# Silu of the deferred experts from Tanh on ScalarE and two products on VectorE, their banks in VectorE's ring

## The chip, the core and the metric

The kernel runs on one core of a Trainium2 chip. The metric is the device time of one execution in microseconds (us), less is better. The core's engines are TensorE (PE in the profile; its weight loads are PEld), VectorE (DVE), ScalarE (ACT) and GpSimd (POOL); SyncE (SP) issues all DMAs here. Each engine works through its own list of instructions in order and waits on semaphores.

## The reference

Four samples of 512 rows by 128 pass through four gated residual blocks. Only the last one is touched by the change: a mixture of 64 experts, the best 8 of them per row, plus two shared ones.

```
def body(acc, p):                                   # for each of 64 routed experts, w1: 128 x 32, w2: 32 x 128
    h = jax.nn.silu(xf @ W1 + B1) @ W2 + B2
    cw = jnp.sum(jnp.where(ti == e, tw, 0.0), axis=-1)    # the row's weight for expert e, 0 if not among its 8
    return (acc + cw[:, None] * h, None)
def shared_mlp(W1, B1, W2, B2):                     # two of them, hidden width 256
    return jax.nn.silu(xf @ W1 + B1) @ W2 + B2
x = x + jnp.tanh(g_ffn[1]) * (routed + shared)
```

Before that block come cross attention to 154 context rows, two layers of local attention with a gelu feed-forward, and a self and cross attention layer with a relu feed-forward. All values are float32.

## The kernel before, in words

Two slots hold two samples at a time: samples 0 and 1 first, then 2 and 3. The experts of samples 0 and 1 are **deferred**: they are computed while samples 2 and 3 go through their attention layers. Samples 2 and 3 compute theirs at once, at the end of the kernel, with another code path that the change leaves alone (L934, `weigh` at L1291).

The hidden units of all experts, turned so that units lie on partitions and the 512 rows along the free dimension, make 20 chunks of 128: chunks 0 to 3 are the shared experts, chunks 4 to 19 the routed ones, four experts of 32 units each. For a deferred sample u and a chunk c:

- PE multiplies the chunk's first weights with the sample's input (`expert_hidden`, L595) into a bank of PSUM.
- ACT applies Silu with the bias (L959) and writes `units[c % 3]` in SBUF.
- For a routed chunk DVE multiplies that by the rows' weights (L1284), which SP has broadcast from DRAM into `ahead[k % 2]`, one DMA for each of four experts (`fill_ahead`, L1628).
- PE multiplies by the second weights and adds up in `moe_psum` (`expert_out`, L605), two steps after the hidden chunk. In the last step the bias of the routed experts is added by one more matmul, ACT scales the sum with the gate (`expert_sum`, L950), PE turns it back (L623), DVE adds x (L1288) and SP stores it.

**The order** is written out once and is the same on all engines. Each stream (slot 0, slot 1, the deferred experts) is a generator of steps, and `turns` (L78) lays down whose step comes next: while samples 2 and 3 are under way, a step of the deferred stream follows about every three steps of the slots. Each engine runs the same sequence of steps, so its place in its own list is fixed; nothing is decided at run time. In step c of the deferred stream PE fills chunk c and takes chunk c-2, ACT does chunk c, DVE multiplies chunk c-1, and SP waits for that product and refills its buffer.

**Banks.** PSUM has eight banks: three in ACT's ring (`act_bank`, L397), four in DVE's (`dve_bank`, L405), one for `moe_psum`. PE takes the banks of a ring in turn. Before it writes a bank it waits until the engine of the ring has emptied the bank's last item, counted by one semaphore per ring, so items of a ring are emptied in order. Hidden chunks are items of ACT's ring. Local attention takes two DVE banks for the scores of a tile, cross attention four.

What else runs in those steps: local attention's scores are masked and their peaks found on DVE (L1111), the negative peaks (L1171, L1224) release eight exponentials on ACT (L847), DVE inverts the sums (L1098), and POOL divides (L1489); PE turns the weights into one bank of each ring, copied by DVE (L1177 or L1230) and ACT (L830). The rotation of queries and keys is L1130 and L1134 on DVE, behind squares on ACT (L858). A feed-forward uses Gelu on ACT (L1001) and a product on DVE (L1358). ACT's table of functions has to hold the function that it applies; the compiler puts ACT_TABLE_LOAD instructions in its list where it has to change.

## Time and profile before

| | |
|---|---|
| three runs | 979.61, 972.08, 977.14 us; median 977.14 |
| profiled execution | 978.57 us, of which the span of instructions is 976.8 us |
| busy, share of the span | PE 75%, DVE 57%, ACT 55%, PEld 49%, POOL 31% |
| mean granted clock of TensorE | 0.868 of full speed |
| ACT_TABLE_LOAD by line | L847 x21, L959 x21, L1001 x8, L838 x2, L1040 x2, L943 x2, L970 x1, L1015 x1; each 1283 ns |
| chain that ended last, share by engine | PE 40%, DVE 26%, ACT 22%, POOL 4%, issue 4% |

A load of the table stands under the line of the instruction that follows it. Busy time says how much an engine did, not that it held up the end; for that the chain of waits is read. It is followed back from the last instruction, at each step to what released it or to the instruction before it on its engine. "issue" is time in which an engine waited for nothing that the profile shows. The profiler doesn't count semaphore and DMA-issuing instructions as busy.

### The profile page before, as it was taken

The numbers are of one execution on the slowest core, as the hardware profiler recorded it, in microseconds if no ns is written. First come the engines' busy times: TensorE is split into PE (matmuls) and PEld (weight loads), VectorE is DVE, ScalarE is ACT, GpSimd is POOL, SyncE is SP. The second block draws the span as 40 slices with busy tenths as digits, with TensorE's granted clock in tenths as the row PEclk, the third lists the DMA queues.
The fourth block names the chain that finished last, engine by engine and source line by source line (L and its number), as shares of the span: only waits on it lengthen the run. The fifth ranks groups of instructions, "written<-read, shape, count | busy, mean of one in ns | idle before, by whom it ended". The sixth has DMA issues, their size and how long they took to land.

```text
span 976.8 us, 15754 instructions
## 1 busy us (share of the span) xinstructions
PE 733.9 (75%) x5368; PEld 479.6 (49%) x5368; DVE 561.6 (57%) x2212; ACT 539.5 (55%) x1347; POOL 300.9 (31%) x296
## 2 busy tenths in 40 slices
PE   5766487868576867577867867876887697878998
PEld 4344355546354655564444544544556455455443
DVE  4785455655565654746864755555665556474543
ACT  4436365565363545435678448577477477754433
POOL 3453313434233122322432523423523312231200
PEclk9877878988787978767999878999898899898999
DMA  8410010110100000021120120130020101102333
GB/s 268 142 39 1 12 39 1 24 27 8 42 1 11 2 1 1 2 74 36 38 71 23 33 60 22 28 82 1 11 60 23 44 22 28 33 12 91 99 103 96
DMA packets 37162, 41.83 MB, mean 43 GB/s; under 512 B 14345, under 2 KB 23771, under 8 KB 36955
## 3 DMA queue, kind: packets, MB, share of 16 engines
q1 hardware_dynamic: 37083, 40.83, 15.0%
q8 instruction: 43, 0.70, 0.3%
q14 instruction: 36, 0.29, 0.1%
HBM read 28.75 MB, written 2.62 MB: 32 GB/s over the span
## 4 chain that ended last, share of the span: by engine, by line
PE 40%; DVE 26%; ACT 22%; POOL 4%; issue 4%; SPq 1%; DMA 1%; DVEq 0%; POOLq 0%; ACTq 0%
ACT work L847 15%; PE act_psum L595 4%; PE moe_psum L605 4%; DVE work L1111 4%; DVE work L1134 3%; PE dve_psum L462 3%; PE dve_psum L431 3%; DVE res_nrm L1089 2%; DVE stats L1080 2%; PE act_psum L696 2%; PE dve_psum L699 2%; PE dve_psum L502 2%; PE act_psum L492 2%; PE act_psum L760 2%; ACT L959 1%
## 5 line engine op out<-in xcount | busy, mean ns | idle before, releaser
L1489 POOL TENSOR_TENSOR work<-work,rinv 128x512 f32<-128x512 f32 (+1 forms) x80 | 84.7, 1076 | 252.6 <-DVE rinv L1098 252.6
L847 ACT ACTIVATE work<-work,nbias,rnorm 128x128 f32<-128x128 f32 x256 | 122.7, 480 | 56.9 <-DVE nbias L1171 56.8
L431 PE MATMUL dve_psum<-wqkv,hTs 128*128 128x512 f32 x128 | 70.3, 676 | 17.7 <-ACT hTs L992 15.9
L1529 POOL TENSOR_TENSOR hT<-hT,work 128x512 f32<-128x512 f32 x32 | 40.6, 1270 | 123.1 <-DVE work L1134 123.0
L830 ACT COPY v_loc<-act_psum 77x512 f32<-77x512 f32 (+2 forms) x72 | 41.8, 582 | 57.2 <-PE act_psum L555 29.7
L1111 DVE CUSTOM_DVE_ANT_0 work<-dve_psum,masks 128x128 f32<-128x128 f32 x256 | 58.6, 284 | 18.4 <-PE dve_psum L462 18.2
L830 ACT COPY hT<-act_psum 128x512 f32<-128x512 f32 (+1 forms) x60 | 31.0, 520 | 68.6 <-PE act_psum L492 36.4
L1130 DVE TENSOR_TENSOR hT<-dve_psum,tab_a 128x512 f32<-128x512 f32 x32 | 22.0, 686 | 80.3 <-ACT res_nrm L858 38.3
L847 ACT ACTIVATE work<-work,nbias 128x154 f32<-128x154 f32 x128 | 52.3, 410 | 23.5 <-DVE nbias L1224 23.5
L492 PE MATMUL act_psum<-work,v_loc 128*64 128x64 f32 x1024 | 44.5, 251 | 25.7 <-DVE work L1177 18.1
L1471 POOL TENSOR_SCALAR rstd<-mv 128x4 f32<-128x4 f32 x36 | 10.1, 280 | 164.6 <-DVE mv L1083 164.6
L492 PEld LDWEIGHTS act_psum<-work,v_loc 128*64 128x64 f32 x1024 | 40.1, 163 | 32.5 <-issue 25.6
L555 PE MATMUL dve_psum<-ident,work 128*77 128x128 f32 x128 | 28.1, 359 | 36.6 <-POOL work L1489 34.5
L1111 DVE CUSTOM_DVE_ANT_0 work<-dve_psum,no_mask 128x154 f32<-128x154 f32 x144 | 37.1, 313 | 27.7 <-PE dve_psum L544 23.4
L502 PE MATMUL dve_psum<-wo,hT 128*128 128x128 f32 x256 | 36.9, 290 | 19.9 <-ACT hT L830 19.9
L462 PE MATMUL dve_psum<-kT,qT 64*64 64x128 f32 x1024 | 43.5, 320 | 8.9 <-DVE work L1134 8.2
L417 PE MATMUL act_psum<-ident,res_nrm 128*128 128x128 f32 x96 | 18.8, 329 | 41.6 <-DVE res_nrm L1089 41.5
L1535 POOL TENSOR_TENSOR v_loc<-v_loc,rnorm 128x512 f32<-128x512 f32 x32 | 33.6, 1072 | 50.9 <-DVE rnorm L1153 50.9
L847 ACT ACTIVATION_READ_ACCUMULATOR work<-work,nbias,rnorm 128x1 f32 x256 | 47.8, 187 | 0.0
L943 ACT ACTIVATE work<-act_psum,cols 128x512 f32<-128x512 f32 x40 | 27.4, 687 | 36.9 <-PE act_psum L595 36.8
L431 PEld LDWEIGHTS dve_psum<-wqkv,hTs 128*128 128x128 f32 x128 | 24.7, 211 | 41.3 <-issue 18.8
L502 PEld LDWEIGHTS dve_psum<-wo,hT 128*128 128x128 f32 x256 | 33.0, 200 | 23.8 <-ACT hT L830 22.9
(211 smaller groups left out, 1929.1 us busy)
## 6 DMA issues: line engine op xcount, KB each, us to landing
ahead<-cwT_dram SPq DMA_DIRECT2D x128, 64.0 KB, 2.0
v_loc<-v_loc SPq DMA_DIRECT2D x24, 256.0 KB, 3.7
kT<-cwT_dram SPq DMA_DIRECT2D x80, 64.0 KB, 2.0
qT<-cwT_dram SPq DMA_DIRECT2D x48, 64.0 KB, 2.0
wqkv<-in_wqkv_dram SPq DMA_DIRECT2D x2, 768.0 KB
res_nrm<-in_x_dram SPq DMA_DIRECT2D x4, 256.0 KB, 3.1
w_m<-in_w_m_dram SPq DMA_DIRECT2D x1, 1024.0 KB, 8.4
v_loc<-v_loc SPq DMA_DIRECT2D x8, 128.0 KB, 3.1
```

What stands on the lines that cost most here:

```text
L431: nc.tensor.matmul(bank[:], h, attn_w[:, k * INNER:(k + 1) * INNER], start=True, stop=True)\
L462: last = nc.tensor.matmul(banks[odd][half * WINDOW:(half + 1) * WINDOW, c * KEYS:(c + 1) * KEYS], qT[u][d, c, at:at + WINDOW], kT[u][d, c, ...
L492: last = nc.tensor.matmul(bank[DH * odd:DH * odd + DH, c * P + half * WINDOW:c * P + (half + 1) * WINDOW], v_loc[u][:, tile, h * DH:(h + 1 ...
L502: last = nc.tensor.matmul(bank[:, 0:D], oT[u][:, c, :], wo[:, l, c, :], start=(c == 0), stop=(c == INNER // P - 1))
L595: nc.tensor.matmul(bank[:], w, given[:], start=True, stop=True).then_inc(act_filled, 1)
L605: nc.tensor.matmul(moe_psum[:], w, units_of, start=(c == 0), stop=False)
L830: nc.scalar.copy(dst, bank[0:n, 0:w]).then_inc(act_emptied, 1)
L847: last = nc.scalar.activation(weights[:, i, :], weights[:, i, :], ACT.Exp, bias=nbias[u][:, b, i:i + 1], scale=scale_of(i), accum_out=sums ...
L1111: return nc.vector.tensor_tensor_reduce(out=weights, in0=bank[:, at:at + width], in1=mask, scale=1.0, scalar=LOWEST, op0=ALU.add, op1=ALU. ...
L1489: nc.gpsimd.tensor_tensor(some, some, by.unsqueeze(2).to_broadcast(list(some.shape)), ALU.mult).then_inc(ready[u], 1)
L1529: nc.gpsimd.tensor_tensor(own, own, partners[u][:, t % 2, k, :], ALU.add).then_inc(turned_ready[u], 1)
L1535: nc.gpsimd.tensor_tensor(k, k, rnorm[u][:, t, HEADS:].unsqueeze(2).to_broadcast([P, HEADS, DH]), ALU.mult)\
```

## The change

Silu(z) = z / 2 * (1 + tanh(z / 2)). For the deferred samples ACT writes tanh(z/2) into `units`, with z/2 from a scale of 0.5 and a bias column halved in the set-up (`half_bias`). DVE makes z * (1 + tanh(z/2)), which is twice Silu, from it and from the bank: for a shared chunk it adds 1 in place and then multiplies by (bank + bias); for a routed chunk it makes (tanh + 1) * weights, and then (bank + bias) times that. The factor of 2 is taken out with half the gate in `expert_sum`, and for that reason the bias matmul is issued twice. The bank now belongs to DVE's ring: it is released by DVE's second product, and ACT reads it without an item of its own. DVE handles chunk c in step c, not c-1, and SP's refill goes by the same step. Samples 2 and 3 keep Silu.

```diff
--- before.py
+++ after.py
@@ -234,6 +234,8 @@
         tab_b = sb("tab_b", [P, LAYERS, TILES, 2, DH])
         sb2_sum = sb("sb2_sum", [P, 1])
         sb2_g = sb("sb2_g", [P, 1])
+        half_bias = sb("half_bias", [P, ROUTED + SHARED])
+        half_gate = sb2_sum
 
 
         x = per_slot("x", [P, TILES, D])
@@ -315,6 +317,11 @@
             at, _ = COLS[name]
             return cols[0:n, at + k:at + k + 1]
 
+        def bias_of(c):
+
+            at = COLS["sb1"][0] + c if c < SHARED else COLS["moe_b1"][0] + c - SHARED
+            return cols[:, at:at + 1], half_bias[:, at - COLS["moe_b1"][0]:at - COLS["moe_b1"][0] + 1]
+
         def row(name, k=0, w=D, n=P):
             at, _ = ROWS[name]
             return rows[0:n, at + k * w:at + k * w + w]
@@ -350,6 +357,7 @@
         logit_ready, expw_ready, cw_ready = sample_sems("logit_ready"), sample_sems("expw_ready"), sample_sems("cw_ready")
         cwT_stored, weighed_ready = sample_sems("cwT_stored"), sample_sems("weighed_ready")
         x_kept, hT_kept = ([sem(f"{name}{u}") for u in range(DEFER)] for name in ("x_kept", "hT_kept"))
+        tanh_done = sem("tanh_done")
         experts_in_loaded = sem("experts_in_loaded")
         ahead_ready = [sem(f"ahead_ready{j}") for j in range(AHEAD)]
         spread_ready = [[sem(f"spread_ready{u}_{k}") for k in range(SPREAD)] for u in SLOTS] * ROUNDS
@@ -610,12 +618,22 @@
                     pe.wait_ge(experts_in_loaded, 16 * (u + 1))
                     for c in range(CHUNKS + 2):
                         if c < CHUNKS:
-                            expert_hidden(u, c, experts_in)
+                            k = c - SHARED
+                            bank = dve_bank(("units", u, c))
+                            w = w_s1[:, c, :] if c < SHARED else w_m1[:, k * P:(k + 1) * P]
+                            nc.tensor.matmul(bank[:], w, experts_in[:], start=True, stop=True).then_inc(dve_filled, 1)
                         if c >= 2:
-                            expert_out(u, c - 2, units[(c - 2) % 3][:])
+                            b = c - 2
+                            if b == 0 and u > 0:
+                                pe.wait_ge(moe_emptied, u)
+                            pe.wait_ge(dve_emptied, dve_item["units", u, b] + 1)
+                            w = w_s2[:, b, :] if b < SHARED else w_m2[:, b - SHARED, :]
+                            nc.tensor.matmul(moe_psum[:], w, units[b % 3][:], start=(b == 0), stop=False)
                         if c == CHUNKS + 1:
                             pe.wait_ge(ahead_ready[0], ahead_fills(u, ROUTED))
-                            nc.tensor.matmul(moe_psum[:], b_m2[:], ahead[0][0:EXPERTS, :], start=False, stop=True).then_inc(moe_filled, 1)
+                            for twice in range(2):
+                                last = nc.tensor.matmul(moe_psum[:], b_m2[:], ahead[0][0:EXPERTS, :], start=False, stop=(twice == 1))
+                            last.then_inc(moe_filled, 1)
                         yield
                     pe.wait_ge(moe_emptied, u + 1)
                     bank = dve_bank(("moe_out", u))
@@ -942,23 +960,26 @@
                         dst, bias = hid[u][:, k % 3, :], col("moe_b1", k)
                     nc.scalar.activation(dst, bank[:], ACT.Silu, bias=bias).then_inc(act_emptied, 1)
 
-                def expert_sum(u, dst):
+                def expert_sum(u, dst, scale):
                     act.wait_ge(moe_filled, u + 1)
                     if u == 0:
                         act.wait_ge(gate_made, 1)
-                        act.wait_ge(set_up, 3)
-                    nc.scalar.activation(dst, moe_psum[:], ACT.Identity, bias=sb2_g[:], scale=gate[:, GF1:GF1 + 1])\
+                    nc.scalar.activation(dst, moe_psum[:], ACT.Identity, bias=sb2_g[:], scale=scale)\
                       .then_inc(moe_emptied, 1)
 
                 def deferred_experts(u):
+
                     yield
                     for c in range(CHUNKS + 2):
                         if c < CHUNKS:
-                            bank = filled(("moe_h", u, c))
-                            bias = col("sb1", c) if c < SHARED else col("moe_b1", c - SHARED)
-                            nc.scalar.activation(units[c % 3][:], bank[:], ACT.Silu, bias=bias).then_inc(act_emptied, 1)
+                            n = dve_item["units", u, c]
+                            act.wait_ge(dve_filled, n + 1)
+                            if u == 0 and c == 0:
+                                act.wait_ge(set_up, 4)
+                            nc.scalar.activation(units[c % 3][:], dve_psum[n % DVE_BANKS][:], ACT.Tanh, bias=bias_of(c)[1], scale=0.5)\
+                              .then_inc(tanh_done, 1)
                         if c == CHUNKS + 1:
-                            expert_sum(u, units[2][:])
+                            expert_sum(u, units[2][:], half_gate[:])
                         yield
                     yield
                     yield
@@ -1048,7 +1069,7 @@
                         if c < CHUNKS:
                             expert_hidden(u, c)
                         if c == CHUNKS + 1:
-                            expert_sum(u, qT[u][:, 0, :])
+                            expert_sum(u, qT[u][:, 0, :], gate[:, GF1:GF1 + 1])
                         if c % PER_STEP == PER_STEP - 1:
                             yield
                     yield
@@ -1271,17 +1292,28 @@
                     nc.vector.tensor_scalar(row("ln3_b"), row("ln3_b"), gate[:, GX1:GX1 + 1], None, ALU.mult)
                     nc.vector.tensor_tensor(sb2_sum[:], col("sb2", 0), col("sb2", 1), ALU.add).then_inc(set_up, 1)
                     dve.wait_ge(set_up, 2)
+                    at = COLS["moe_b1"][0]
+                    nc.vector.tensor_scalar(half_bias[:], cols[:, at:at + ROUTED + SHARED], 0.5, None, ALU.mult)
                     nc.vector.tensor_scalar(sb2_g[:], sb2_sum[:], gate[:, GF1:GF1 + 1], None, ALU.mult).then_inc(set_up, 1)
+                    dve.wait_ge(set_up, 3)
+                    nc.vector.tensor_scalar(half_gate[:], gate[:, GF1:GF1 + 1], 0.5, None, ALU.mult).then_inc(set_up, 1)
 
                 def deferred_experts(u):
                     yield
                     for c in range(CHUNKS + 2):
-                        k = c - 1 - SHARED
-                        if 0 <= k < ROUTED:
-                            rows_of, weights = units[(c - 1) % 3][:], ahead[k % AHEAD][:]
-                            dve.wait_ge(ahead_ready[k % AHEAD], ahead_fills(u, k))
-                            dve.wait_ge(act_emptied, act_item["moe_h", u, c - 1] + 1)
-                            nc.vector.tensor_tensor(rows_of, weights, rows_of, ALU.mult).then_inc(weighed_ready[u], 1)
+                        if c < CHUNKS:
+                            k, unit = c - SHARED, units[c % 3][:]
+                            bank = filled(("units", u, c))
+                            dve.wait_ge(tanh_done, u * CHUNKS + c + 1)
+                            if c < SHARED:
+                                link(nc.vector.tensor_scalar(unit, unit, 1.0, None, ALU.add))
+                            else:
+                                dve.wait_ge(ahead_ready[k % AHEAD], ahead_fills(u, k))
+                                nc.vector.scalar_tensor_tensor(out=unit, in0=unit, scalar=1.0, in1=ahead[k % AHEAD][:],
+                                                               op0=ALU.add, op1=ALU.mult).then_inc(weighed_ready[u], 1)
+                                dve.wait_ge(weighed_ready[u], k + 1)
+                            nc.vector.scalar_tensor_tensor(out=unit, in0=bank[:], scalar=bias_of(c)[0], in1=unit,
+                                                           op0=ALU.add, op1=ALU.mult).then_inc(dve_emptied, 1)
                         yield
                     bank = filled(("moe_out", u))
                     dve.wait_ge(ahead_ready[1], ahead_fills(u, ROUTED))
@@ -1631,7 +1663,7 @@
 
                     sp.wait_ge(hT_kept[u], 16)
                     if u > 0:
-                        sp.wait_ge(act_filled, act_item["moe_h", u - 1, CHUNKS - 1] + 1)
+                        sp.wait_ge(dve_filled, dve_item["units", u - 1, CHUNKS - 1] + 1)
                     sp.dma_start(experts_in[:], hT_dram[u]).then_inc(experts_in_loaded, 16)
                     sp.wait_ge(cwT_stored[u], 16)
                     if u > 0:
@@ -1642,7 +1674,7 @@
                     fill_ahead(1)
                     yield
                     for c in range(CHUNKS + 2):
-                        k = c - 1 - SHARED
+                        k = c - SHARED
                         if 0 <= k < ROUTED:
                             sp.wait_ge(weighed_ready[u], k + 1)
                             if k + AHEAD < ROUTED:
```

## Rows read from the trace of the kernel before

**Rows 1.** windows: us; busy us of PE, PEld, DVE, ACT, POOL; clock, DMA

```profile
436.00:852.00 416.00, 322.75 (x2410) 205.95 (x2410) 248.67 (x958) 269.79 (x622) 135.46 (x127) 0.90 0.14 36
```

**Rows 2.** chain of waits, 436 to 852 us: start, us, engine, names, line

```profile
by line: ACT work L847 17.8%; DVE work L1134 4.5%; issue 3.9%; DVE work L1111 3.4%; ACT L959 3.4%; PE act_psum L595 3.2%; PE moe_psum L605 2.8%; PE act_psum L492 2.6%; DVE res_nrm L1089 2.4%; DVE stats L1080 2.3%; PE dve_psum L431 2.0%; DVE
...
469.50 0.81 DVE units L1284
...
507.46 1.28 ACT L959
...
510.51 1.28 ACT L847
...
797.95 0.57 DVE units L1284
```

**Rows 3.** groups of ACT, whole span: count, busy us, mean ns, idle before

```profile
L959 ACT ACTIVATE units<-act_psum,cols 128x512 f32<-128x512 f32 x40 | 27.5, 687 | 15.6 <-PE act_psum L595 15.2
...
L847 ACT ACT_TABLE_LOAD x21 | 26.9, 1283 | 0.4
L959 ACT ACT_TABLE_LOAD x21 | 26.9, 1283 | 0.4
```

**Rows 4.** timeline of ACT, 5 to 20 us: start, us, instruction, idle before

```profile
7.21 0.20 ACT L970 ACTIVATE gate<-rows 128x4 f32<-128x4 f32 x1 [0.98 <-DMA rows<-in_rows_dram]
...
18.92 0.42 ACT L838 ACTIVATE work<-work,nbias 128x154 f32<-128x154 f32 x1 [0.93 <-DVE nbias L1318]
```

**Rows 5.** groups of DVE, whole span, shapes kept apart

```profile
L1284 DVE TENSOR_TENSOR units<-ahead,units 128x512 f32<-128x512 f32 x32 | 25.2, 789 | 0.1
...
L1089 DVE TENSOR_SCALAR res_nrm<-y,mv,rstd 128x128 f32<-128x128 f32 x48 | 13.4, 342 | 8.3 <-POOL rstd L1472 7.8
...
L1358 DVE SCALAR_TENSOR_TENSOR qT<-dve_psum,cols,work 128x512 f32<-128x512 f32 x16 | 11.9, 750 | 37.3 <-PE dve_psum L699 25.1 <-ACT work L1001 12.1
```

**Rows 6.** timeline of DVE, two linked instructions of the root

```profile
478.24 0.18 DVE L1149 TENSOR_SCALAR rnorm<-sumsq 128x32 int32<-128x32 int32 x1
478.45 0.19 DVE L1151 TENSOR_TENSOR root<-rnorm 128x32 f32<-128x32 f32 x1
```

**Rows 7.** timelines of DVE and ACT, 723 to 738 us

```profile
723.24 0.69 DVE L1284 TENSOR_TENSOR units<-ahead,units 128x512 f32<-128x512 f32 x1
725.73 0.69 DVE L1363 TENSOR_TENSOR y<-dve_psum,res_nrm 128x512 f32<-128x512 f32 x1 [1.80 <-PE dve_psum L706]
...
735.46 0.29 DVE L1111 CUSTOM_DVE_ANT_0 work<-dve_psum,masks 128x128 f32<-128x128 f32 x1 [0.73 <-PE dve_psum L462]
...
726.26 1.28 ACT L959 ACT_TABLE_LOAD   x1
727.56 0.69 ACT L959 ACTIVATE units<-act_psum,cols 128x512 f32<-128x512 f32 x1
...
729.58 0.49 ACT L847 ACTIVATE work<-work,nbias,rnorm 128x128 f32<-128x128 f32 x1
...
737.84 0.49 ACT L847 ACTIVATE work<-work,nbias,rnorm 128x128 f32<-128x128 f32 x1
```

**Rows 8.** timelines of DVE, ACT and SP, 759 to 764 us

```profile
759.48 0.68 DVE L1284 TENSOR_TENSOR units<-ahead,units 128x512 f32<-128x512 f32 x1
...
761.66 0.69 ACT L959 ACTIVATE units<-act_psum,cols 128x512 f32<-128x512 f32 x1 [0.46 <-PE act_psum L595]
...
760.18 1.70 SPq L1628 DMA_DIRECT2D ahead<-cwT_dram  x4
763.73 0.67 SPq L1692 DMA_DIRECT2D v_loc<-y  x1
```

**Rows 9.** timeline of DVE, two rotations that wait for ACT's squares

```profile
465.89 0.69 DVE L1130 TENSOR_TENSOR hT<-dve_psum,tab_a 128x512 f32<-128x512 f32 x1 [0.92 <-ACT res_nrm L858]
...
537.07 0.69 DVE L1130 TENSOR_TENSOR hT<-dve_psum,tab_a 128x512 f32<-128x512 f32 x1 [5.40 <-ACT work L858]
```

**Rows 10.** timeline of PE at 485.8 us, with its wait

```profile
485.84 1.55 PE L431 MATMUL dve_psum<-wqkv,hTs 128*128 128x512 f32 x3 [1.79 <-DVE peak L1111]
```

## The prediction

> **What bounds the kernel now.** I read the windows first, to see where the touched work lies. The deferred experts fill the stretch from 436 to 852 us; there ACT is busy 269.8 of 416 us, DVE 248.7 and PE 322.8 [rows 1]. No engine is full, so the chain of waits comes next [rows 2]. It changes engine every few microseconds: the exponentials of L847 lead, then the rotation, masks and statistics on DVE. Two things in it belong to the change. ACT_TABLE_LOAD at L959 has 3.4% of 416 us, 14.1 us, which is eleven loads of 1.28; four more at L847 (first at 510.51) and one at L1015 make sixteen. The old DVE product at L1284 is on it eight times, first at 469.50, last at 797.95. The stretch after 852 us is PE's, with the last samples' experts; the change doesn't enter it but for the last unit.
>
> The groups of ACT show 21 loads ahead of Silu at L959 and 21 ahead of the exponentials at L847, 1283 ns each [rows 3]. All loads, from the small table above, are 58.
>
> **What the change removes.** Tanh at 7.21 us is followed by the first Exp at 18.92 with no load between them [rows 4]; one table serves both. So the 21 loads at L959 go. Of those at L847, eight follow a Gelu and stay, thirteen go; two at L838, one of two at L1040 and the one at L1015 go too. That is 38 x 1.283 = 48.8 us of ACT. From a load's start to the start of the next instruction is 1.30 us, as at 726.26 and 727.56 [rows 7]. The sixteen on the chain are 16 x 1.30 = 20.8 us, the most that can be won directly. The Trainium skill (ScalarE: Activation LUTs, What ACT_TABLE_LOAD costs) adds a drain and says about 2.66 us a switch, by which those sixteen would be worth an estimated 42.6 us. The rows contradict it, since the Silu starts 1.30 us after the load does.
>
> Tanh itself costs ACT what Silu did, 687 ns [rows 3]: same shape, same bias operand.
>
> **What it adds on DVE.** Before, a routed unit takes 0.6 us, start to next start, as the piece at 797.95 shows [rows 2]; a shared unit takes nothing. After, a routed unit has two linked instructions. The first (two operands in SBUF, immediate scalar) is nearest the old product, 0.69 where undisturbed [rows 7]; its mean is 0.79 [rows 5]. The second reads a bank with a column as scalar, as L1358 does: 0.75. Between instructions linked by a semaphore lie 0.03 us [rows 6], while the 0.6 above means that unlinked ones overlap by 0.09. So 0.69 + 0.04 + 0.66 = 1.39 to the next start, 0.79 more than now, 32 times: 25 us. A shared unit has an add of 1.0 over 512 columns in SBUF, which the trace doesn't show: at least the 0.34 of 128 columns at L1089 [rows 5], at most 0.75. I take 0.45, nearer the short end since it has one operand. With link and second product 1.15, eight times: 9 us. DVE gains 34 us of occupied time in the stretch, to 283 of 416, a little above where ACT was.
>
> **What it moves.** This decides it. The step order is fixed. Before, DVE handled unit c-1 in step c, and never waited. Now it handles unit c in step c, behind ACT's Tanh of the same step. I set each L1284 beside the Silu of its step: in 19 of 30 steps DVE stood there before the Silu had ended, by 3.4 us on average, 6.9 at most (723.24 against 728.25 is one of them [rows 7], 759.48 against 762.35 another [rows 8]). DVE must now stand idle there, and what queues behind it is the other samples' work. Walking the chain from step to step, with u for the deferred sample and c for its unit:
>
> - Units 3 to 8 of u=0 (459 to 500 us): DVE is the chain [rows 2]. Shared unit 3 (1.15) and unit 4 (1.39) are new there and fill an idle 0.92 [rows 9], +1.6; four routed ones add 4 x 0.79 = 3.2. Together **+4.8**.
> - Two of u=1, units 6 and 7: DVE reaches the place at 723.24, ACT is in exponentials until 726.2 [rows 7]. Tanh takes the load's slot and ends at 726.95, the unit at 728.4. The ff_out add, on the chain at 725.73, goes to 728.4, 2.7 late; with it the scores that ACT waits for at 729.58. Eight exponentials later Tanh 7 ends at 737.5, the unit at 739.0, the bank copy 0.6 on, and the scores of 735.46 start at about 739.8, so that the exponentials of 737.84 begin at 740.95. **+3.1**, with the loads on that path already taken off.
> - Unit 9 of u=1: the product starts at once now and waits for Tanh at 762.35 then. SP issues the four broadcasts after the product and only then the shift of y, on the chain at 763.73 [rows 8]. Four issues take 1.7 us: 763.05 + 0.1 + 1.7 to 764.85 for the shift by that, and 763.85 + 1.1 + 0.3 + 0.2 = 765.4 by DVE's own queue of unit, norm and add. **+1.7**.
> - Four other routed units on the chain (the last four of the eight, at 518.97, 562.47, 771.77 and 797.95): 4 x 0.79 = **+3.2**. Units 0 and 4 of u=1, between rotation and scores or norm: **+1.1** and **+1.4**.
> - Steps where a load leaves the chain. In units 17 and 19 of u=0 and 8 of u=1 the bank copy for PE, or the scores, stands behind the unit, so 1.3 goes and 1.4 comes: **0**. Before a rotation, as at 537.07 where DVE idled 5.40 [rows 9], 0.4, 0.4 and 0.7 are left of 1.3. At unit 10 1.0 of 2.6, at 14 and 15 of u=1 0.4 and 0.2 of 5.2, at unit 18 1.3. Together **-4.4**.
> - One more matmul of the biases for each deferred sample. L605's, of the same size, have 2.8% of 416 us of the chain [rows 2] in eleven visits, 1.06 each. At the end of a sample's units PE waits for others, so 0, at most +2.1. Two small DVE instructions in the set-up and one more wait are paid once, 0.2 to 0.3 us, beside L0's attention: 0.
>
> Sum: 4.8 + 3.1 + 1.7 + 3.2 + 2.5 - 4.4 = **+10.9**. The span of 976.8 goes to 987.7, the profiled execution of 978.57 to 989.5. That execution lies 1.4 above the median of the three, 977.14, so the median goes to **988**.
>
> POOL gets later inputs where DVE stalls, counted in the steps above; it was busy for only 135 of the 416 us [rows 1]. SP's waits for the weighed unit keep their step.
>
> **The rivals.** The bound between change and no change is about 1% here.
>
> A, **faster**: ACT is the bound. All sixteen loads come off in full, -20.8, and the waits on DVE fall into its own idle time, leaving only its longer work: 4.8 + 3.2 + 2.5 = 10.5. That gives 977 - 10.3 = 967. For it speaks the weight of L847 in the chain [rows 2]; against it that at 726.26 and 734 the chain runs through what stands behind the unit. It decides if a stall upstream makes DVE late anyway, so that Tanh is already there. Chance 0.18. By the skill's 2.66 us it would end near 945; with the rows against that figure, it gets 0.01 of this.
>
> B, **balance**: DVE, delayed by its first extra 5 us, arrives later at each next unit and waits less. Of 3.1 + 1.7 + 2.5 some 5 us then vanish: 983, within 1%. Chance 0.24.
>
> C, **the ring**: the unit sits in DVE's four banks from its matmul to its second product. PE already stops for a DVE bank, 1.79 us at 485.84 [rows 10]. Masks of cross attention need four banks at once. If twelve units from 765 to 852 us stop PE by 0.7 to 1.8 us more than I walked, that is 8 to 22, mid 14: 1002. ACT's ring of three is freed in turn, which speaks against it. It decides once PE's wait for the bank outlasts DVE's own queue. Chance 0.11.
>
> D, **the loads stay**, since the tables are placed otherwise than after the first Tanh: then DVE's 15.3 come without the 4.4, and the two at 737 and 729 come back, 2.6: 995. Chance 0.03.
>
> **How the numbers follow.** My forecast has 0.44. Its own range is 982 to 995: below, half of +10.9; above, 0.3 us dearer units (the shared add at 0.75, a first product at 0.79 mean) and the matmuls, +7. Three tenths of it lie under 987 (977 + 1%). Slower: 0.44 x 0.7 + 0.11 + 0.03 = 0.45. Within 1%: 0.13 + 0.24 = 0.37. Faster: 0.18. The range that leaves out 2 in 10 reaches into A below and to C's middle above: 966 to 1002.
>
> **What would show it.** Loads fall from 58 to about 20, ACT's busy time in the stretch by 49 us, DVE's rises by 30 to 35. DVE should show idle time ahead of the first product that ends with a Tanh, some 40 us in all, above all at units 6, 7 and 9 of u=1. L1284's successor should be on the chain more than eight times. I am wrong if that idle time is under 15 us, or if the exponentials of the local attention start earlier by more than the stalls; then A or B holds. PE idle for DVE banks growing by over 10 us would be C.

## The result: 1.4% slower, as forecast, from larger parts than forecast

Five runs of the changed kernel gave 984.86, 990.50, 990.52, 989.87 and 990.11 us, median 990.11. Five of the kernel before on the same chip gave a median of 975.2. The ratio is 1.0139, 95% interval [1.0108, 1.0171], about 13.6 us (the two medians lie 14.9 apart). The prediction was 988, its forecast's own range 982 to 995, and the forecast sum +10.9.

The profiled execution of after is the 984.86 one, span 983.1 us, so its trace is some 5 us better than the typical run; that of before was 978.57 (span 976.8), 3.4 above its median. The granted clock of TensorE was 0.883 in this execution and 0.865 to 0.873 in the other four of after. Where the two traces are laid side by side below, only +6.3 us has to be found, and each trace is one execution.

The windows of after and, for the same bounds, of before (us; busy us of PE, PEld, DVE, ACT, POOL with counts; clock; DMA). Set beside [rows 1], both reach eight microseconds further, since after's deferred units run to 856 us.

```profile
436.00:860.00 424.00, 324.97 (x2405) 207.51 (x2404) 281.04 (x1020) 221.44 (x592) 135.51 (x127) 0.91 0.14 36
```

```profile
436.00:860.00 424.00, 329.74 (x2464) 212.01 (x2464) 254.40 (x986) 274.68 (x640) 137.51 (x130) 0.90 0.14 36
```

In these 424 us ACT has lost 53.2 us of work, DVE has gained 26.6 (32.7 over the whole span), and the sum of both is smaller; the kernel is slower all the same. The engines' shares can't say why.

The groups of ACT after (count, busy us, mean ns, idle before), which answer to [rows 3]. The loads are down to 8 + 8 + 2 + 1 + 1 = 20; Tanh costs what Silu cost.

```profile
L979 ACT ACTIVATE units<-dve_psum,half_bias 128x512 f32<-128x512 f32 x40 | 27.3, 683 | 19.7 <-PE dve_psum L624 19.6
...
L1022 ACT ACT_TABLE_LOAD x8 | 10.3, 1283 | 0.1
L865 ACT ACT_TABLE_LOAD x8 | 10.3, 1283 | 0.1
```

The groups of DVE after, which answer to L1284 of [rows 5]:

```profile
L1315 DVE SCALAR_TENSOR_TENSOR units<-dve_psum,cols,units 128x512 f32<-128x512 f32 x40 | 30.0, 751 | 1.4
...
L1312 DVE SCALAR_TENSOR_TENSOR units<-units,ahead 128x512 f32<-128x512 f32 x32 | 25.5, 796 | 43.6 <-ACT units L979 32.2 <-PE dve_psum L624 6.6 <-issue 4.8
```

L1284 sat 0.1 us idle in all. Its successor L1312 sits 43.6. The waits of DVE and ACT (us in total, times, longest) name what is being waited for, and the wait that follows from it:

```profile
ACT work L865 <- DVE nbias L1192: 82.9, 28, 6.0
...
DVE units L1312 <- ACT units L979: 32.2, 11, 5.9
...
DVE units L1309 <- ACT units L979: 8.3, 3, 4.1
```

In before the first row's counterpart read:

```profile
ACT work L847 <- DVE nbias L1171: 56.8, 23, 5.1
```

So DVE stands 40.5 us in 14 places for the Tanh of its own step. ACT stands 26.1 us longer for the negative peaks, half of its saved work. Not all of that is DVE's new wait. In the first experiment below, Tanh alone, DVE's list is as before, and the row reads

```profile
ACT work L847 <- DVE nbias L1171: 71.1, 27, 5.1
```

So 14.3 of the 26.1 us are saved loads turned into waiting. The other 11.8 come with DVE's earlier step and longer unit (77.9 with Tanh and the step).

**Where along the kernel the time goes.** For each of the 40 units I took the start of its activation in before, and how much later it starts in another trace (us, u the sample, c the unit):

| unit | before | after | Tanh alone | step alone | Tanh and step | after with loads |
|---|---|---|---|---|---|---|
| u=0 c=0 | 440.65 | -3.2 | +1.5 | +0.3 | -0.4 | +1.2 |
| u=0 c=3 | 456.41 | -4.0 | +1.5 | +0.3 | -0.4 | +1.9 |
| u=0 c=9 | 495.88 | +1.4 | +1.5 | +2.6 | +0.6 | +10.3 |
| u=0 c=19 | 614.49 | +0.5 | -7.9 | +6.9 | -5.1 | +13.9 |
| u=1 c=0 | 662.25 | +0.5 | -9.0 | +9.3 | -5.8 | +17.0 |
| u=1 c=5 | 709.80 | +3.6 | -10.5 | +11.9 | -5.0 | +20.8 |
| u=1 c=6 | 727.56 | +1.7 | -12.7 | +11.2 | -7.4 | +19.8 |
| u=1 c=8 | 752.42 | +4.5 | -12.8 | +16.5 | -6.2 | +25.4 |
| u=1 c=10 | 764.71 | +9.3 | -12.6 | +19.8 | -4.5 | +28.6 |
| u=1 c=19 | 848.79 | +5.6 | -18.1 | +19.3 | -9.1 | +30.3 |

After enters the stretch 3.2 us ahead. The change isn't what does it: over the first 200 us the granted clock was 0.88 against 0.85, and the same 1060 matmuls kept PE busy for 130.3 us against 135.3. After leaves the stretch 5.6 behind: 8.9 us. It loses in the two places that the walk had named: c=3 to c=9 of u=0, 5.3 us, and c=6 to c=10 of u=1, 7.5 us. A second trace shows the same. That of the last experiment below, the changed kernel with one small matmul fewer per deferred sample (span 987.5), enters at +0.4, loses 4.6 and 7.5 in the two places and leaves at +10.1.

The timelines of DVE and ACT in after, 757 to 773 us, are the second place (start, us, instruction, idle before). They answer to [rows 8].

```profile
757.70 0.69 DVE L1312 SCALAR_TENSOR_TENSOR units<-units,ahead 128x512 f32<-128x512 f32 x1 [2.17 <-ACT units L979]
758.42 0.75 DVE L1315 SCALAR_TENSOR_TENSOR units<-dve_psum,cols,units 128x512 f32<-128x512 f32 x1
...
766.71 0.28 DVE L1202 TENSOR_TENSOR y<-dve_psum,y 128x128 f32<-128x128 f32 x1
769.87 0.69 DVE L1312 SCALAR_TENSOR_TENSOR units<-units,ahead 128x512 f32<-128x512 f32 x1 [2.88 <-PE dve_psum L624]
770.60 0.75 DVE L1315 SCALAR_TENSOR_TENSOR units<-dve_psum,cols,units 128x512 f32<-128x512 f32 x1
771.26 1.11 DVE L1110 TENSOR_SCALAR res_nrm<-y,mv,rstd 128x128 f32<-128x128 f32 x4
772.29 0.28 DVE L1202 TENSOR_TENSOR y<-dve_psum,y 128x128 f32<-128x128 f32 x1
...
769.09 0.69 ACT L979 ACTIVATE units<-dve_psum,half_bias 128x512 f32<-128x512 f32 x1 [0.46 <-PE dve_psum L624]
```

The same three instructions on DVE in before:

```profile
759.28 0.28 DVE L1181 TENSOR_TENSOR y<-dve_psum,y 128x128 f32<-128x128 f32 x1
...
760.26 1.11 DVE L1089 TENSOR_SCALAR res_nrm<-y,mv,rstd 128x128 f32<-128x128 f32 x4
763.41 0.29 DVE L1181 TENSOR_TENSOR y<-dve_psum,y 128x128 f32<-128x128 f32 x1 [2.04 <-PE dve_psum L502]
```

Between the add at 766.71 and the norm at 771.26 lie 4.55 us, 0.98 before. The trace puts the idle 2.88 down to PE's bank, but the Tanh ends at 769.78, 0.09 before the product starts: it is the same wait. The next add, which SP's shift of y waits for, comes 5.58 us after the first, 4.13 in before. So 1.45 us is lost here; the prediction had 1.7.

### The profile page after: what moved, and what is told of

It is laid out like the page before. It is cut to its first block and busy times, and to the rows that moved or that the text cites. A ratio compares the mean times of both kernels' runs of the same rounds, so it can differ in the third digit from the quotient of the medians.

```text
span 983.1 us, 15784 instructions
## 1 busy us (share of the span) xinstructions
PE 728.6 (74%) x5372; PEld 478.1 (49%) x5372; DVE 594.3 (60%) x2262; ACT 489.4 (50%) x1309; POOL 301.4 (31%) x296
## 3 DMA queue, kind: packets, MB, share of 16 engines
q1 hardware_dynamic: 37083, 40.83, 14.9%
## 5 line engine op out<-in xcount | busy, mean ns | idle before, releaser
L1503 POOL TENSOR_SCALAR rstd<-mv 128x4 f32<-128x4 f32 x36 | 10.5, 293 | 161.8 <-DVE mv L1104 161.7
L510 PE MATMUL dve_psum<-wo,hT 128*128 128x128 f32 x256 | 39.0, 300 | 26.5 <-ACT hT L848 19.1
L470 PE MATMUL dve_psum<-kT,qT 64*64 64x128 f32 x1024 | 42.0, 312 | 13.9 <-DVE work L1155 13.2
L1312 DVE SCALAR_TENSOR_TENSOR units<-units,ahead 128x512 f32<-128x512 f32 x32 | 25.5, 796 | 43.6 <-ACT units L979 32.2
```

The lines of the kernel that those rows point to most:

```text
L470: last = nc.tensor.matmul(banks[odd][half * WINDOW:(half + 1) * WINDOW, c * KEYS:(c + 1) * KEYS], qT[u][d, c, at:at + WINDOW], kT[u][d, c, ...
L510: last = nc.tensor.matmul(bank[:, 0:D], oT[u][:, c, :], wo[:, l, c, :], start=(c == 0), stop=(c == INNER // P - 1))
```

## Experiments

The theory: the loads are worth less than the sum of unit work and wait. Rivals were that ACT's loads come off in full (A), that DVE catches up (B), and that DVE's banks hold PE up (C). All ratios are to the kernel before, run on the same chip as the experiment; its median was 975.3 us (Tanh alone, the step alone, both, the first second-instruction run), 978.44 (its repeat, all but the ring, the own bank with 0 and 2 steps) and 975.7 (the rest). A difference between two ratios is uncertain by 0.5 to 0.6%, some 5 to 6 us.

### Tanh alone

```
-    nc.scalar.activation(units[c % 3][:], bank[:], ACT.Silu, bias=bias).then_inc(act_emptied, 1)
+    nc.scalar.activation(units[c % 3][:], bank[:], ACT.Tanh, bias=bias).then_inc(act_emptied, 1)
```

> The kernel before with Tanh written where Silu was and nothing else, so the output leaves out the product with z: the loads' worth alone. The theory of the prediction (the loads on the chain are worth up to 20.8 us, and DVE's work and waits eat them) expects 38 loads less, ACT 49 us less busy, and 955 to 962 us, 1.4 to 2.1% under the kernel before; DVE doesn't wait for this ACT work, so nothing is given back. The theory that the loads were hidden beside other work expects under 0.5%. The rival that ACT was the bound (A) expects 2% or more.

Measured: 960.31 us, 0.984 [0.9793, 0.9887], -15.0 us, with 20 loads left. DVE's product, a unit behind, waits no more than before:

```profile
L1284 DVE TENSOR_TENSOR units<-ahead,units 128x512 f32<-128x512 f32 x32 | 25.3, 789 | 0.1
```

So 38 loads of 48.8 us are worth 15 us where nothing new waits. The sixteen on the chain had been priced at 20.8 as the most that can be won directly; some three quarters of it is what came. A's 2% or more lies at the edge of the interval.

### The step alone

```
-    k = c - 1 - SHARED
+    k = c - SHARED
...
-        rows_of, weights = units[(c - 1) % 3][:], ahead[k % AHEAD][:]
+        rows_of, weights = units[c % 3][:], ahead[k % AHEAD][:]
...
-        dve.wait_ge(act_emptied, act_item["moe_h", u, c - 1] + 1)
+        dve.wait_ge(act_emptied, act_item["moe_h", u, c] + 1)
```

SP's refill moves with it, as in the change. Silu and the single product stay.

> The kernel before with one thing changed: DVE multiplies chunk c in step c and not c-1, with Silu, its loads, one product and ACT's ring as they were. The wait alone. The theory of the prediction expects DVE idle ahead of L1284 for 45 to 65 us in all (19 of 30 steps late by 3.4 us on average) and a time 0.6 to 2% over the kernel before, most of it at units 6, 7 and 9 of the second deferred sample. The theory of rival B, that DVE is late anyway once it is delayed, expects under 15 us idle and no change within 0.4%.

Measured: 997.01 us, 1.0208 [1.0156, 1.0259], +21.7 us, for the same instructions in the same number. The product's group:

```profile
L1284 DVE TENSOR_TENSOR units<-ahead,units 128x512 f32<-128x512 f32 x32 | 25.5, 796 | 62.3 <-ACT units L959 62.2
```

Idle time of DVE ahead of it goes from 0.1 to 62.3 us. About a third of that reaches the end. The time is a hair over the 2% expected at most, and the place was expected wrongly: from c=5 to c=10 of u=1 the table has 7.9 us, not most of the loss; the rest is spread over the stretch. The clock isn't the cause of more than a small part. The execution with clock 0.869 took 994.22, while those of before with 0.869 took 973.16 to 981.28.

### Both together

The two edits above in one kernel.

> The kernel before with Tanh for Silu (the product with z is left out) and DVE's one product in step c: loads off and the wait on, without the second product and with ACT's ring. The theory of the prediction expects DVE idle ahead of L1284 for 30 to 45 us, and a time between the two parts: 0.3 to 1.2% under the kernel before, at least 0.8% over Tanh alone. If the wait costs nothing it is as fast as Tanh alone; if the wait is the whole of the change's cost, it is 1% or more over the kernel before.

Measured: 969.37 us over ten runs, 0.9933 [0.9904, 0.9961].

```profile
L1284 DVE TENSOR_TENSOR units<-ahead,units 128x512 f32<-128x512 f32 x32 | 25.0, 780 | 43.0 <-ACT units L959 42.9
```

Against Tanh alone the wait costs 0.9933/0.984, or 9.1 us. Against the step alone the loads are worth 27.6 us. The two don't add: 27.6 against 15.0 is more than the uncertainty, and DVE's idle time ahead of the product fell from 62.3 to 43.0 us with the loads. My reading, which no run tests by itself: a load ahead of an activation that DVE is waiting for holds up both engines. Up to here the change would have been a gain.

### A second DVE instruction alone

The longer DVE work at the old place, a unit behind ACT, with Silu and the loads kept. A first version took as the second instruction a maximum of the unit with itself:

```
+    if k < 0:
+        link(nc.vector.tensor_scalar(unit, unit, 1.0, None, ALU.mult))
+    else:
+        nc.vector.tensor_tensor(unit, ahead[k % AHEAD][:], unit, ALU.mult).then_inc(weighed_ready[u], 1)
+        dve.wait_ge(weighed_ready[u], k + 1)
+    nc.vector.scalar_tensor_tensor(out=unit, in0=unit, scalar=1.0, in1=unit,
+                                   op0=ALU.mult, op1=ALU.max).then_inc(unit_done, 1)
```

> The kernel before with DVE's work made as long as in the changed kernel, at its old place (chunk c-1 in step c) and in ACT's ring: a second linked instruction on each of the 40 units, a maximum of the unit with itself, and a linked product by 1 for the eight shared ones. The longer work alone. The theory of the prediction expects DVE busy 30 to 34 us more and 5 to 11 us more time, 0.5 to 1.1%. If DVE has room in this stretch, as its 60% busy time suggests, under 0.3%.

Measured: 994.6 us, 1.0188 [1.0146, 1.0229], over the 1.1% expected at most. But its group shows that it isn't the change's load:

```profile
L1292 DVE SCALAR_TENSOR_TENSOR units<-units 128x512 f32<-128x512 f32 x40 | 41.0, 1025 | 1.4
```

It averages 1025 ns, where the change's product, with one operand in PSUM, takes 751. The timelines show where that comes from: 25 of the 40 took 0.69 us, and the 15 others, 1.41 to 1.65 us, all overlapped an instruction of POOL on 128x512, as here:

```profile
484.34 1.72 POOL L1538 TENSOR_TENSOR v_loc<-v_loc,work 128x512 f32<-128x512 f32 x1
484.97 1.64 DVE L1292 SCALAR_TENSOR_TENSOR units<-units 128x512 f32<-128x512 f32 x1
```

That run overstates the work by 11 us. It was repeated with an instruction that reads the unit once:

```
+    nc.vector.tensor_reduce(sb2_sum[:], unit, AX.X, ALU.max).then_inc(unit_done, 1)
```

> As the run with the second product alone, but the second linked instruction is a maximum over the unit's 512 columns into one spare column, with one operand in SBUF. The two-operand instruction took 1025 ns on average there, against 751 for the changed kernel's second product, so that run was about 11 us of DVE too dear. Here the second instruction should take 0.65 to 0.75 us without stretching, DVE's added work 30 to 34 us as in the change. The theory of the prediction, corrected by that run (18.4 us for 45 us of added work), expects 10 to 14 us, 1.0 to 1.4% over the kernel before; its first sizing was 0.5 to 1.1%.

Measured: 988.66 us, 1.0127 [1.0077, 1.0177], +12.4 us at 978.44.

```profile
L1292 DVE TENSOR_REDUCE sb_sum<-units 128x1 f32<-128x512 f32 x40 | 27.4, 686 | 1.4
```

Fifteen of these reductions ran beside such an instruction of POOL too, all in 0.69 us. This is the price of DVE's added work by itself, within the 10 to 14 us expected and over the 0.5 to 1.1% of the first sizing, yet with an uncertainty of 5 us not to be told from the 10.5 us that the prediction's terms of pure work add up to (4.8 + 3.2 + 2.5).

### All but the ring

Tanh, the earlier step and two linked DVE instructions, but the units in ACT's ring: the two edits above and the last one together.

> Tanh for Silu (the product with z is left out), DVE in step c, and two linked DVE instructions on each unit (product with the weights or with 1, then the maximum over the columns), but the hidden chunk in ACT's ring as before: the changed kernel without its move to DVE's ring. The theory that the ring costs nothing expects 1.0 to 1.6% over the kernel before, the same as the changed kernel within 0.4%. Rival C, that PE's waits for DVE's banks are a part of the cost, expects 0.6% or less. The theory that loads, wait and work add up expects -1.6 + 0.9 + 1.2 = 0.5% and leaves 0.9% to the ring.

Measured: 987.79 us, 1.0122 [1.0072, 1.0173]. The changed kernel stands at 1.0139. Moving the units to DVE's ring, with the true operands, costs nothing that shows: 0.2%, uncertain by 0.6%.

```profile
L1289 DVE TENSOR_TENSOR units<-ahead,units 128x512 f32<-128x512 f32 x32 | 25.4, 794 | 43.8 <-ACT units L961 41.6 <-issue 2.1
```

Against Tanh and step, the second instruction costs 1.0122/0.9933, or 1.9%; at its old place, without waits, 1.3%. The difference of 0.6% has an uncertainty of about 0.8%, so whether the work grows dearer behind the wait stays open.

### Five banks for DVE

```
-    ACT_BANKS, DVE_BANKS = 3, 4
+    ACT_BANKS, DVE_BANKS = 2, 5
```

> The changed kernel with DVE's ring at five banks and ACT's at two (four and three before); nothing else. Theory: banks are not what the change lost, so the ratio to before stays at 1.010 to 1.018; PE's waits for DVE's banks fall by a few us, those for ACT's rise by as much. Rival C (the ring of DVE's banks holds PE up): at least 0.8% less than the changed kernel, ratio below 1.006. A third case, a dearer one: a ring of two on ACT stops the exponentials' matmuls, ratio above 1.02.

Measured: 997.36 us, 1.022 [1.0175, 1.0264], the third case and not the theory's. PE's waits for units in DVE's banks are gone but for 0.6 us, from 11.6 in after, and a new one for ACT's ring is there. Waits of PE (us, times, longest), here and in after:

```profile
PE act_psum L485 <- ACT hT L848: 20.6, 10, 3.7
```

```profile
PE act_psum L485 <- ACT hT L848: 3.1, 1, 3.1
```

The trade of one bank loses 0.8%. The run can't tell what the fifth bank wins from what ACT's third one was worth; it shows only that the first is less than the second.

### A bank of the units' own, DVE later

The obvious repair: keep the Tanh, but let DVE come to it later. Its sum z then has to stay in PSUM, so the units get the one bank that ACT's ring gives up.

```
+    unit_psum = ctx.enter_context(nc.psum_tensor("unit_psum", [P, 512], F32))
...
-    ACT_BANKS, DVE_BANKS = 3, 4
+    ACT_BANKS, DVE_BANKS = 2, 4
+    LATER = 0
...
+    pe.wait_ge(unit_done, u * CHUNKS + c)
+    nc.tensor.matmul(unit_psum[:], w, experts_in[:], start=True, stop=True).then_inc(unit_filled, 1)
```

DVE takes a unit LATER steps of the slots after its Tanh.

> The changed kernel with one PSUM bank of its own for the deferred units, outside both rings, and two banks instead of three in ACT's ring; DVE still handles chunk c in step c. SP's refill goes one step later, as in the kernel before. If the ring costs nothing: as the changed kernel, 1.0 to 1.8% over the kernel before. If PE's waits for DVE's ring are a part: 0.8% or less over it. It is the reference for the run with DVE's units two slot steps later.

> As the run with the units' own bank, but DVE handles a unit two slot steps later in its list, some 5 us, so that Tanh is done when DVE gets there; all work and results are as in the changed kernel. The theory of the prediction expects DVE's idle time ahead of the first product to fall from about 40 us to under 8, and 0.5 to 1.2% less time than with the units' own bank and no delay, because the wait in order was worth that. If the longer work is the whole cost and the wait is taken back elsewhere: no change within 0.3%. PE may wait for the one bank instead, which would show as idle time of PE ahead of the next hidden chunk.

> The changed kernel with a PSUM bank of its own for the units (ACT's ring two), DVE handling the unit one slot step later than its Tanh. With no shift this form took 1.0223 of before's time, with two steps 1.046. Theory (the wait only changes its engine): DVE's idle time ahead of the first product falls from 50.5 us to under 20, PE's wait for the single bank rises from about 5 to 30 or more, ratio between the two, 1.025 to 1.04. Rival (one step is enough for the Tanh and short enough for the bank): ratio 1.010 to 1.018, lower than with no shift.

| steps later | us | ratio | DVE idle ahead of L1325 | PE and PEld idle for the bank |
|---|---|---|---|---|
| 0 | 998.98 | 1.0223 [1.018, 1.0267] | 44.6 | 1.5, 4.8 |
| 1 | 1001.44 | 1.0258 [1.0216, 1.0301] | 5.0 | 19.6, 24.0 |
| 2 | 1021.8 | 1.046 [1.0417, 1.0502] | 0.0 | 48.0, 55.7 |

The waits with two steps:

```profile
ACT units L992 <- PE unit_psum L638: 61.5, 26, 7.5
PEld unit_psum L638 <- DVE units L1328: 55.7, 22, 4.6
...
PE unit_psum L638 <- DVE units L1328: 48.0, 20, 4.3
```

At no shift this form equals the kernel with five banks, above both cases of its expectation, which hadn't counted the bank taken from ACT. The two kernels have the ring of two in common, and PE's wait for ACT's copies at that place (20.4 us here, 20.6 there, 3.1 in after), so I take the 0.8% for the price of that ring. With the shift DVE's wait vanishes as meant, 44.6 to 5.0 to 0.0, and stands again on PE, which can't fill the single bank. One step more costs nothing clear of the noise (1.0258 against 1.0223), two cost 2.3%. My expectation that two steps would be 0.5 to 1.2% cheaper than none failed by its sign: I had counted the wait that goes and not what the held bank stops. The later expectation, that the wait only changes its engine, held at one step in the ratio and in DVE's idle time; the 30 us or more for PE were too many, 19.6 on the matmuls and 24.0 on their weight loads. A kernel that avoids the wait without taking a bank from ACT wasn't tried.

### The loads back in the changed kernel

```
-    nc.scalar.activation(units[c % 3][:], dve_psum[n % DVE_BANKS][:], ACT.Tanh, bias=bias_of(c)[1], scale=0.5)\
+    nc.scalar.activation(units[c % 3][:], dve_psum[n % DVE_BANKS][:], ACT.Silu, bias=bias_of(c)[1], scale=0.5)\
```

> The changed kernel with Silu back in Tanh's place on ACT, everything else as changed (so the unit computed is not the reference's: silu of the halved sum, plus 1, times z). It gives back the 38 table loads and keeps both DVE instructions, the wait and DVE's ring. Theory (part sums): with one product and a wait, taking the loads off was worth 997.0 - 969.4 = 27.6 us; with no wait it was worth 15.0. The changed structure waits, so the loads are worth 18 to 28 us here: ratio to before 1.033 to 1.042. Rival (saturation: once DVE carries the longer unit, ACT's loads lie in DVE's shadow): under 10 us, ratio below 1.025. ACT_TABLE_LOADs 58, DVE's idle time ahead of the first product 60 us or more by the first theory, about 45 by the rival.

Measured: 1010.33 us, 1.0346 [1.0305, 1.0388], 58 loads. DVE idles longer ahead of the first product, 59.8 us, a hair under the 60 expected:

```profile
L1312 DVE SCALAR_TENSOR_TENSOR units<-units,ahead 128x512 f32<-128x512 f32 x32 | 25.4, 794 | 59.8 <-ACT units L979 44.9 <-PE dve_psum L624 6.3 <-issue 5.7
```

In the changed structure the loads are worth 1.0346/1.0139, 2.0% or 20 us: between the 15.0 with no wait and the 27.6 with the wait and a single product. At 20 us, uncertain by 5, it can't be told from either by itself, but the saturation rival, under 10, is out.

### One matmul of the biases

```
-    for twice in range(2):
-        last = nc.tensor.matmul(moe_psum[:], b_m2[:], ahead[0][0:EXPERTS, :], start=False, stop=(twice == 1))
+    last = nc.tensor.matmul(moe_psum[:], b_m2[:], ahead[0][0:EXPERTS, :], start=False, stop=True)
```

> The changed kernel with the matmul of the biases done once, not twice, for each deferred sample (so the biases are halved in the result). Theory: at the end of a sample's units PE waits for others, so the second one cost nothing: ratio to before 1.010 to 1.018, within 0.3% of the changed kernel. Rival: the two lie on the path at 1.06 us each, 2.1 us or 0.2% less; this run could not tell 0.2% from nothing by its time, so its PE waits at that place decide.

Measured: 989.08 us, 1.0131 [1.0088, 1.0173], the changed kernel's time within the interval. In after the group reads

```profile
L635 PE MATMUL moe_psum<-ahead,b_m 64*128 64x512 f32 x8 | 4.0, 615 | 0.0
```

where this run has 4 records and 2.2 us, so the two added for the deferred samples are 1.8 us of PE's work. ACT's wait for the sum is 2.1 us in after and 1.3 here, in one place: one of the two is seen there, by 0.8 us. Whether that reaches the end the time can't tell.

## Why the prediction was right, point by point

**The loads.** Their number is exact: 58 to 20. ACT's busy time from 436 to 860 us falls by 53.2 us, forecast 49. "The most that can be won directly", 20.8, held against 15.0 with nothing else changed, and not where DVE waits, 27.6. The Trainium skill (ScalarE: Activation LUTs, What ACT_TABLE_LOAD costs) puts a switch at about 2.66 us with its drain, by which the sixteen on the chain would be worth an estimated 42.6 us. This case disagrees: the Silu starts 1.30 us after its load does (726.26 and 727.56 us in before), and the gains were 15.0 us from the loads alone and 27.6 with DVE waiting.

**The work on DVE.** Forecast +34 us of occupied time, 30 to 35 of busy time in the stretch; there the busy time rose by 26.6 (28.6 in the forecast's own 416 us), over the whole span by 32.7. The unit in the trace: first product 0.69 where undisturbed (757.70), second at 758.42, next instruction at 759.09: 1.39 from start to start, as computed. The shared add's median is 0.426, assumed 0.45; its mean is 0.585. The 26.6 falls short since the two windows don't hold the same other work; the units' own groups grew by 30.0 + 25.5 + 4.7 - 25.2 = 35.0. Its price, 10.5 in the terms of the sum, is 12.4 alone and 18.6 beside Tanh and the wait, uncertain by some 5 and 6.

**The wait.** Forecast "some 40 us" of idle time ahead of the first product, ended by a Tanh; measured 40.5 in 14 places. Of u=1 units 6, 8, 9 and 10 wait, 3.59, 2.17, 2.88 and 2.25 (that of unit 9 stands outside the 40.5, put down to PE). Unit 7 stands 1.34 idle, put down to issue. This was the step that decided the sign, and it came from comparing two starts in the trace of before ([rows 7, 8]), not from any share.

**The sizes along the way.** u=0, c=3 to 9: +4.8 forecast, +5.3 seen. u=1, c=0 to 5: +2.5 forecast, +3.0 seen. From c=5 to c=6 1.8 us come back. Units 6 and 7: +3.1, against +2.8 from the start of c=6 to c=8. Unit 9: +1.7, against 1.45 at the place itself and 1.8 from the start of c=9 to that of c=10. From the start of c=6 to that of c=10 the forecast had 4.8 (3.1 + 0 + 1.7), and 7.5 are seen. What is missing shows between c=8 and c=9, where 2.9 us are lost, in both traces. I had put unit 8 at 0, its load against its longer work, without a wait for its Tanh; DVE waits 2.17 us there.

**What was off and cancelled.** Loads and waits together were +0.4 in the sum (3.1 + 1.7 - 4.4); the run with both and one product shows -0.67%, -6.5 us. The work was +10.5; in that company it is 1.9%, +18.6. Two errors of 7 and 8 us with opposite signs, each uncertain by 3 to 6. By single runs, loads that were worth -4.4 in the sum gave -15.0, waits that were 3.1 + 1.7 cost 9.1, and work that was 10.5 cost 18.6. The terms don't map one to one: the -4.4 and the two waits have some of the longer unit in them. But every part was larger than forecast. My reading of it is that a chain of one execution prices the steps that are on it, and when they change others step in; the run with the earlier step alone, where the loss is spread over more places than the walk had, speaks for that, but no run tests it. That the sum came out near the measured time owes something to luck.

**The rivals.** A is out: the loads gave 15 us, but with a result of +13.6 the rest of the change took 28.6. B would have needed DVE to wait less as it grows later; the total wait came out as forecast, 40.5, and the longer unit didn't shorten it (idle time ahead of the first product: 43.0 us with Tanh and the step, 43.8 with the second instruction added, 43.6 in after). In the last ten units after does win back 3.6 us of the shift (9.3 to 5.6), but that isn't B: Tanh alone wins 5.5 there, and Tanh and step 4.6. C's own sign did come: PE's idle time for DVE's banks grew by more than the 10 us that was to mean C. For banks that units held it is 11.6 us in after, where before had none, and for banks of scores 7.6 against 7.4. Most of it is

```profile
PE dve_psum L510 <- DVE units L1315: 4.6, 2, 2.3
PE dve_psum L552 <- DVE units L1315: 3.3, 2, 3.1
PE dve_psum L738 <- DVE units L1315: 2.7, 2, 1.7
```

C is out all the same, since its price of 14 us isn't there: without the ring, and so without these waits, the kernel is only 0.2% faster, uncertain by 0.6%. The sign was badly chosen, for idle time of PE isn't time at the end. D didn't occur. Whether L1284's successor is on the chain more than eight times stays open, because the chain of after is followed back only to 766 us; from there to 852 us it is on it five times, before's product twice.

The parts in one line, in us: loads -15.0; the wait, once the loads are gone, +9.1; the second instruction +18.6; the ring and the true operands, +1.6 with no significance. Together +14.3 against +13.6 measured. That they add up is no proof of the split: each term is the step from one kernel to the next, and in another order the terms differ (the loads 15.0, 20 or 27.6).

No kernel here beats the one before while computing the whole. With the wait avoided, the parts would by an estimate from the single runs be -1.6 + 1.3 = -0.3%, less than a run can show, and the attempt to avoid it cost a bank that ACT needed.

## What to carry to other kernels

An instruction moved one step earlier in an in-order list can cost more than the work that it saves elsewhere: compare the start of the instruction in the trace with the end of what it will wait for, place by place, and look at what is queued behind it. Work taken off one engine and given to another is worth what lies on the path of each: here 48.8 us saved on ACT gave 15, or 27.6 where DVE waited for it, and 35 us added on DVE took 12 to 19. Before repairing a wait by holding a buffer longer, ask who fills that buffer next.

## What the runs showed of the hardware that I had not expected

- The stretching of DVE's instructions follows POOL. On 128x512 float32 the one that reads the same SBUF tile twice took 0.69 us in 25 of 40 cases and 1.41 to 1.65 in the 15 that overlapped a 128x512 instruction of POOL. The reduction, which reads one tile, took 0.69 in all 40, with 15 overlapping. The product with one operand in PSUM took 751 ns in all 40, with 11 overlapping. The forms (min/median/max ns, first and last start) in after show how far the ones in SBUF spread:

```profile
L1315 DVE SCALAR_TENSOR_TENSOR units<-dve_psum,cols,units x40: 750/751/752, 438.9 to 855.9; 128x512 f32<-128x512 f32 x40
L1312 DVE SCALAR_TENSOR_TENSOR units<-units,ahead x32: 659/692/1637, 462.8 to 855.2; 128x512 f32<-128x512 f32 x32
...
L1309 DVE TENSOR_SCALAR units<-units x8: 397/426/1380, 438.5 to 700.6; 128x512 f32<-128x512 f32 x8
```

- Of the 32 of L1312, the 9 above 0.72 us all overlapped a 128x512 instruction of POOL; 2 others overlapped one by half a microsecond and weren't stretched. No run took POOL's work away, so this is shown by coincidence in time alone.
- The same 38 table loads were worth 15.0 us with nothing waiting behind the activation, 27.6 with DVE waiting and one product, and 20 in the changed kernel; only the first two are clear of each other.
